# Attention with 128-row table products, signs split on ScalarE, and high halves read in place

## The chip, the cores and the metric

The kernel runs on one core of a Trainium2 chip. The metric is the device time of one execution in microseconds (us), the median over several runs. In the text PE is TensorE, PEld its weight loads, DVE is VectorE, ACT is ScalarE, POOL is GpSimd and SP is SyncE. A q behind an engine's name (PEldq, DVEq) means its instruction queue: the part that handles waits, register operations and the issue of instructions.

## The reference

One layer of a model that fuses image and text tokens: a tokenizer (sines and cosines of the image), attention, and a soft mixture of experts, for 8 batches of 640 tokens (512 image, 128 text) of width 192. The change is in the attention, which is linear attention with 4 sets of queries (G = 4), 12 heads and 64 dimensions:

```python
def _phi(x):
    return jnp.concatenate([jax.nn.relu(x), jax.nn.relu(-x)], axis=-1)
...
q = jnp.einsum('gbhnd,gde->gbhne', q, Wt) + bt[:, None, None, None, :]
q = jax.nn.gelu(q, approximate=False)
q = _ln(q, gt[:, None, None, None, :], betat[:, None, None, None, :])
qf = _phi(q) / jnp.sqrt(jnp.float32(2 * DH))
kf = _phi(k)
kv = jnp.einsum('bhnd,bhnm->bhdm', kf, v)
out = jnp.einsum('gbhnd,bhdm->gbhnm', qf, kv)
ksum = kf.sum(axis=2)
norm = jnp.einsum('gbhnd,bhd->gbhn', qf, ksum)
out = out / (norm[..., None] + 1e-06)
out = out.transpose(1, 3, 0, 2, 4).reshape(b, n, G * INNER)
fused = jax.nn.gelu(_ln(out @ Wf + bf, gf, betaf), approximate=False)
return fused @ Wo + bo
```

The features of a head are 128 numbers: 64 of the positive part and 64 of the negative part. For each batch and head there is a table `kv` of 128 x 64, and `ksum` as its 65th column (KVW = 65).

## The kernel before

The kernel is written engine by engine; each engine has its own order of work, and semaphores tie them together. Stages follow each other: tokenizer, attention weights, keys and values, attention, experts. Wherever a product needs nearly full precision, an f32 operand is split into two bf16 parts, `hi` and `lo` (the rest), and the product is made of three: hi x hi, hi x lo and lo x hi.

Keys and values (`keys_and_values`): for each of 40 tiles of 128 tokens (5 a batch) and each half of the heads, ACT makes the two signs of the key features (`kf`, layout head, sign, dimension), DVE and POOL split them, and `accumulate` on PE sums the tables in `ps_kv`. A product there has 128 tokens as rows and 64 feature columns (one head, one sign); two heads use the two column halves of the array. At a batch's end `store_kv` on ACT and DVE writes both parts of the tables to `kvs`, which holds all 8 batches: [batch, part, pair of heads, sign, 65], with one head of the pair in partitions 0 to 63 and the other in 64 to 127.

Attention (`attend`): 40 tiles of 128 tokens, and for each 6 octets j = 0 to 5 of 8 (set, head) pairs. Every engine walks through slots (tile, j) and in each slot does parts of several octets, so that the work is pipelined over some six slots. The first two tiles and the last are written out, the 37 between are a loop over a register `t`. An engine's order in one slot is written by hand:

- PE: `queries(j+3)` (5 products of 512 columns), at j = 2 `turn_x`, `turn_octet(j)` (4 transposes of the scaled queries into `ps_t`), at j = 4 `turn_y` (6 transposes), `attend_octet(j-1)` (the table products), `fuse(j-2)` (24 products of 384 columns), `turn_outputs(j-1)`, at j = 5 `project_out` (18 products).
- ACT: `high_outputs(j-2)`, `gelu(j+3)`, at j = 2 `move_x`, `features(j)`, `square(j+2)`, at j = 4 `fused_gelu` twice.
- DVE: `center(j+2)`, `low_outputs(j-2)`, `sum_q(j+3)`, `divide(j-1)`, `scale_q(j+1)`, `high_phi(j)`, `sum_squares(j+2)`, and parts for the tile at some j.
- POOL: `rstd_q(j+1)`, at j = 3 `rstd_y`, at j = 5 `low_ys`, `low_phi(j)`.
- SP: for each tile one DMA that copies the batch's tables from `kvs` to the fixed place `kv_now`.

The features of an octet go through these steps: `features` (ACT, from `ps_t` to `phi`, f32, one operation for each sign and each query set in the octet; octets 1 and 4 hold two sets), `high_phi` (DVE, copy to bf16), `low_phi` (POOL, the rest), `attend_octet` (PE). In `ps_t` two heads share the partitions, one in 0 to 63 and one in 64 to 127, so a table product has 64 rows, and the two heads of a pair run in the two row halves of the array: 4 pairs x 2 signs x 3 parts x 2 heads = 48 products of 65 columns. PE waits there for `phi_hi_done`, `phi_lo_done` and `o_done`, and for `kv_in` at j = 0.

The tokenizer already reads the high half of an f32 value as its upper 16 bits, every other bf16 element (`high`), as weights at L154.

## Time and profile before

| | |
|---|---|
| median of 3 runs | 2717.93 us (2717.76 to 2718.2) |
| profiled execution | 2718.29 us |
| its span, first to last instruction | 2716.4 us |
| mean granted TensorE clock, share of full speed | 0.96 |
| PE busy / DVE busy | 94% / 91% |
| ACT busy / POOL busy | 51% / 50% |

Busy times are those of instructions in execution; register, branch and semaphore operations in the queues are not counted. Products on PE are pipelined: one begins before the one ahead has ended, so the distance of their starts tells the pace, not their duration. In a timeline, a line with xN is N instructions of one kind that follow each other. A wait is put down to what came last.

### The profile page before, as it was taken

To read this page: it belongs to the slowest core of one execution; us is meant where nothing else is said; L and a number is where in the kernel's file an instruction comes from. 1 tells how busy PE (TensorE), PEld (TensorE's weight loads), DVE (VectorE), ACT (ScalarE), POOL (GpSimd) and SP (SyncE) were. 2 spreads that over 40 slices of the span, in tenths; PEclk is the share of its full clock that TensorE was granted. 3 is DMA by queue.
4 is the path that set the end of the run, shared out by engine and by line. 5 is a ranking of instruction groups with operands and counts; after the bars stand their busy time and mean duration, and the time that the engine had idled before them with its cause. 6 is when DMAs were issued, how large, how long until landed. Compare 5 with 4: busy or idle time off the path is not lost. (4 is left out here: it accounts for less than half of the span.)

```text
span 2716.4 us, 74938 instructions
## 1 busy us (share of the span) xinstructions
PE 2542.6 (94%) x29336; PEld 1722.5 (63%) x29336; DVE 2483.3 (91%) x3770; ACT 1392.7 (51%) x2302; POOL 1350.4 (50%) x1019
## 2 busy tenths in 40 slices
PE   4999999788879999999999999999999999999577
PEld 2777777555546666666666666666666666666335
DVE  6999999888889999999999999999999999999583
ACT  5676766555545545545444545545444544554231
POOL 0000000555556666666666666666666766666210
PEclk8999999899989999999999999999999999999765
DMA  7321210211100000000000000000000000000001
GB/s 153 96 51 36 51 35 18 62 36 41 35 7 14 10 8 12 6 12 6 12 6 12 6 12 12 6 12 6 12 6 12 6 12 12 6 12 7 6 0 58
DMA packets 45139, 62.39 MB, mean 23 GB/s; under 512 B 4416, under 2 KB 36160, under 8 KB 44760
## 3 DMA queue, kind: packets, MB, share of 16 engines
q1 hardware_dynamic: 43928, 61.07, 8.5%
q8 instruction: 40, 0.66, 0.1%
q10 hardware_dynamic: 1152, 0.51, 0.1%
q14 instruction: 19, 0.16, 0.0%
HBM read 41.66 MB, written 3.93 MB: 17 GB/s over the span
## 5 line engine op out<-in xcount | busy, mean ns | idle before, releaser
L1231 POOL TENSOR_TENSOR phi_lo<-phi,phi_hi 128x1024 bf16<-128x1024 f32 x240 | 511.2, 2130 | 459.8 <-DVE phi_hi L1112 459.8
L1022 ACT ACTIVATE o_hi<-ps_u 128x512 bf16<-128x512 f32 x240 | 143.3, 597 | 705.1 <-PE ps_u L927 705.1
L941 PE MATMUL ps_y<-staging,o_hi 128*128 128x384 bf16 x1920 | 470.4, 327 | 9.6 <-DVE o_lo L1134 1.9
L941 PE MATMUL ps_y<-staging,o_lo 128*128 128x384 bf16 x1920 | 469.0, 326 | 0.0
L941 PE MATMUL ps_y<-wf_lo,o_hi 128*128 128x384 bf16 x1920 | 468.9, 326 | 0.0
L1224 POOL TENSOR_TENSOR q_ssq<-q_ssq,half 128x8 f32<-128x8 f32 x240 | 405.9, 1691 | 18.8
L1013 ACT ACTIVATE phi<-ps_t,betat,gt 128x512 f32<-128x512 f32 (+1 forms) x640 | 384.8, 672 | 0.8 <-PE ps_t L896 0.8
L1090 DVE SCALAR_TENSOR_TENSOR shared<-q_sum,shared 128x512 f32<-128x512 f32 x240 | 374.3, 1559 | 1.4
L154 PE MATMUL acc<-w_b,feat 128*128 128x384 bf16 x1728 | 295.5, 331 | 42.8 <-DVE w_b L266 39.4
L154 PEld LDWEIGHTS acc<-w_b,feat 128*128 128x128 bf16 x1728 | 168.5, 99 | 158.3 <-DVE w_b L266 40.0
L941 PEld LDWEIGHTS ps_y<-staging,o_lo 128*128 128x128 bf16 x1920 | 187.8, 98 | 124.2
L941 PEld LDWEIGHTS ps_y<-wf_lo,o_hi 128*128 128x128 bf16 x1920 | 187.6, 98 | 124.5
L941 PEld LDWEIGHTS ps_y<-staging,o_hi 128*128 128x128 bf16 x1920 | 169.3, 98 | 118.7 <-issue 15.4
L252 DVE TENSOR_TENSOR f_low<-feat 128x4608 bf16<-128x4608 f32 x48 | 237.7, 4951 | 1.3 <-ACT feat L196 1.3
L369 POOL MEMSET half<- 128x40 f32 x1 | 0.1, 131 | 476.7 <-POOLq L101 476.7
L997 ACT ACTIVATE shared<-ps_a 128x512 f32<-128x512 f32 x240 | 143.5, 598 | 179.1 <-PE ps_a L880 176.1
L1112 DVE CAST phi_hi<-phi 128x1024 bf16<-128x1024 f32 x240 | 219.6, 915 | 0.0
L914 PE MATMUL ps_o<-kv_now,phi_hi 64*128 64x65 bf16 x7680 | 212.8, 191 | 1.7 <-issue 1.7
L914 PEld LDWEIGHTS ps_o<-kv_now,phi_hi 64*128 64x128 bf16 x7680 | 183.9, 94 | 42.1 <-issue 42.1
L914 PE MATMUL ps_o<-kv_now,phi_lo 64*128 64x65 bf16 x3840 | 202.8, 190 | 0.0
L1085 DVE TENSOR_REDUCE q_sum<-shared 128x8 f32<-128x512 f32 x240 | 162.5, 677 | 20.7 <-ACT shared L997 19.5
L914 PEld LDWEIGHTS ps_o<-kv_now,phi_lo 64*128 64x128 bf16 x3840 | 180.6, 94 | 0.0
(218 smaller groups left out, 5664.4 us busy)
## 6 DMA issues: line engine op xcount, KB each, us to landing
kv_now<-kvs SPq DMA_DIRECT2D x40, 390.0 KB, 2.6
xt<-in_x_dram SPq DMA_DIRECT2D x32, 320.0 KB, 5.5
wf_f<-in_wf_dram SPq DMA_DIRECT2D x24, 384.0 KB, 3.2
xt<-in_x_dram SPq DMA_DIRECT2D x32, 256.0 KB, 6.0
out_dram<-h SPq DMA_DIRECT2D x8, 480.0 KB, 2.9
staging<-in_wq_t_dram SPq DMA_DIRECT2D x1, 3072.0 KB, 11.0
staging<-in_tok_w_dram SPq DMA_DIRECT2D x12, 192.0 KB, 8.8
staging<-in_kv_w_dram SPq DMA_DIRECT2D x1, 1536.0 KB, 15.3
```

The costliest lines, as they stand in the source:

```text
L154: last = nc.tensor.matmul(acc[:, u, t, 0:2 * DIM], high(ring(u, i))[:, k, t * P:(t + 1) * P], w_b[:, i, k, :], start=i == 0 and k == 0, st ...
L252: nc.vector.tensor_tensor(low[:, r], feat[:, r], high(r), ALU.subtract).then_inc(low_ready, 1)
L914: last = nc.tensor.matmul(ps_o[:, a, i * KVW:(i + 1) * KVW], feature[rows, j % 2, sign, i * P:(i + 1) * P], kv_now[rows, table, pair, sign ...
L941: last = nc.tensor.matmul(ps_y[:, n, 0:HC], lhs, w[part][:, c, n * HC:(n + 1) * HC], start=c == 0 and lhs is oh and part == 'wf_hi', stop= ...
L997: nc.scalar.activation(q[:, j % RING].rearrange("p h d -> p (h d)"), ps_a[:, bank[f"oct{j}"], 0:OC], ACT.Gelu).then_inc(s["gelu_done"], 1)
L1013: last = nc.scalar.activation(phi[:, j % 2, sign, a * P:b * P], ps_t[:, a * P:b * P], ACT.Relu, bias=w['betat'][:, sign, g:g + 1], scale=w ...
L1022: nc.scalar.activation(o_hi[:, j % 2], ps_u[:, 0:OC], ACT.Copy).then_inc(s["o_hi_done"], 1)
L1085: nc.vector.tensor_reduce(total[:, j % 2], q[:, j % RING], AX_X, ALU.add).then_inc(s["q_sum"], 1)
L1090: nc.vector.scalar_tensor_tensor(out=q[:, j % RING], in0=total[:, j % 2].unsqueeze(2).broadcast_to([P, OCT, DH]), scalar=1.0 / DH, in1=q[: ...
L1112: nc.vector.tensor_copy(phi_hi[:, j % 2], phi[:, j % 2]).then_inc(s["phi_hi_done"], 1)
L1224: nc.gpsimd.tensor_tensor(ssq[:, j % 2], ssq[:, j % 2], w['half'][:, 0:OCT], ALU.pow).then_inc(s["q_rstd"], 1)
L1231: nc.gpsimd.tensor_tensor(phi_lo[:, j % 2], phi[:, j % 2], phi_hi[:, j % 2], ALU.subtract).then_inc(s["phi_lo_done"], 1)
```

## The change

Five edits that belong together:

- One head's two signs lie in the 128 partitions instead of two heads' one sign. A table is [128 features, 65] for each head, in `kv_hi` and `kv_lo` (two tensors now, [batch, head, 65]). `accumulate` takes 128 feature columns in one product (18 a call instead of 36), `attend_octet` takes 128 rows (24 instead of 48).
- `features` writes each sign to its own half of the partitions. An operation now covers one head of the pairs (64 partitions) and one sign: 4 for each query set in the octet, of the same number of columns as before.
- `phi_hi` is no tensor of its own: it is `phi` read as bf16, every other element. `high_phi` on DVE and its semaphore go; `low_phi` waits for `phi_done`, and `features` waits for `attended` of two octets earlier.
- `kv_now` and its DMA go. The products read `kv_hi[:, b, hd, :]` and `kv_lo[:, b, hd, :]`, with `b` worked out from the tile; in the looped tiles it is a run-time value.
- `o` is laid out by halves of the octet, and `divide` and `turn_outputs` index it so.

```diff
@@ keys_and_values: accumulate
-                    for j in range(HH // 2):
-                        for sign in range(2):
-                            for n, (k, v) in enumerate(((kf_hi, v_hi), (kf_hi, v_lo), (kf_lo, v_hi))):
-                                for side in range(2):
-                                    c = 2 * j + sign
-                                    last = nc.tensor.matmul(
-                                        ps_kv[side * DH:(side + 1) * DH, hf, c * KVW:(c + 1) * KVW],
-                                        k[:, m, 2 * j + side, sign, :], v[:, m, 2 * j + side, :],
...
+                    for j in range(HH):
+                        for n, (k, v) in enumerate(((kf_hi, v_hi), (kf_hi, v_lo), (kf_lo, v_hi))):
+                            last = nc.tensor.matmul(ps_kv[:, hf, j * KVW:(j + 1) * KVW],
+                                                    k[:, m, j].rearrange("p s d -> p (s d)"), v[:, m, j, :],
...
@@ attend: tensors
-        kv_now = sb("kv_now", [P, 2, HP, 2, KVW], BF16)
-        phi = sb("phi", [P, 2, 2, PAIRS * P], F32)
-        phi_hi = sb("phi_hi", [P, 2, 2, PAIRS * P], BF16)
-        phi_lo = sb("phi_lo", [P, 2, 2, PAIRS * P], BF16)
-        o = sb("o", [P, PAIRS, 2, DH], F32)
+        phi = sb("phi", [P, 2, PAIRS, 2, P], F32)
+        phi_hi = phi[:, :, :, :, :].bitcast(BF16)[:, :, :, :, 1::2]
+        phi_lo = sb("phi_lo", [P, 2, PAIRS, 2, P], BF16)
+        o = sb("o", [P, 2, PAIRS, DH], F32)
@@ attend: the block of SP with kv_now's DMA goes
@@ attend: attend_octet
-                    pe.wait_ge(s["phi_hi_done"], count(tile, j, NO))
                     pe.wait_ge(s["phi_lo_done"], count(tile, j, NO))
                     if (n := earlier(tile, j, NO, 1)) is not None:
                         pe.wait_ge(s["o_done"], n)
-                    if j == 0:
-                        pe.wait_ge(s["kv_in"], 16 * count(tile, 0, 1))
-                    for i in range(PAIRS):
-                        pair = (PAIRS * j + i) % HP
-                        for sign in range(2):
-                            for n, (feature, table) in enumerate(((phi_hi, 0), (phi_hi, 1), (phi_lo, 0))):
-                                for a in range(2):
-                                    rows = slice(a * DH, (a + 1) * DH)
-                                    last = nc.tensor.matmul(
-                                        ps_o[:, a, i * KVW:(i + 1) * KVW],
-                                        feature[rows, j % 2, sign, i * P:(i + 1) * P], kv_now[rows, table, pair, sign, :],
...
+                    b = batch_of(tile.t)
+                    for i in range(OCT):
+                        hd = (OCT * j + i) % HEADS
+                        c = i % PAIRS
+                        out = ps_o[:, i // PAIRS, c * KVW:(c + 1) * KVW]
+                        ph, pl = (v[:, j % 2, i // 2, i % 2, :] for v in (phi_hi, phi_lo))
+                        nc.tensor.matmul(out, ph, kv_hi[:, b, hd, :], start=c == 0, stop=False, skip_group_check=True)
+                        nc.tensor.matmul(out, ph, kv_lo[:, b, hd, :], start=False, stop=False, skip_group_check=True)
+                        last = nc.tensor.matmul(out, pl, kv_hi[:, b, hd, :], start=False, stop=c == PAIRS - 1,
+                                                skip_group_check=True)
@@ attend: features
-                        act.wait_ge(s["phi_hi_done"], n)
-                        act.wait_ge(s["phi_lo_done"], n)
-                    for sign in range(2):
-                        for g, a, b in groups(j):
-                            last = nc.scalar.activation(
-                                phi[:, j % 2, sign, a * P:b * P], ps_t[:, a * P:b * P], ACT.Relu,
-                                bias=w['betat'][:, sign, g:g + 1], scale=w['gt'][:, sign, g:g + 1])
+                        act.wait_ge(s["attended"], n)
+                    for g, a, b in groups(j):
+                        for head in range(2):
+                            rows = slice(head * DH, (head + 1) * DH)
+                            for sign in range(2):
+                                last = nc.scalar.activation(
+                                    phi[sign * DH:(sign + 1) * DH, j % 2, a:b, head, :],
+                                    ps_t[rows, a * P:b * P].rearrange("p (i n) -> p i n", n=P), ACT.Relu,
+                                    bias=w['betat'][rows, sign, g:g + 1], scale=w['gt'][rows, sign, g:g + 1])
@@ attend: high_phi goes, low_phi
-                    nc.vector.tensor_copy(phi_hi[:, j % 2], phi[:, j % 2]).then_inc(s["phi_hi_done"], 1)
...
-                    pool.wait_ge(s["phi_hi_done"], count(tile, j, NO))
+                    pool.wait_ge(s["phi_done"], count(tile, j, NO))
@@ early_fusion_kernel
-            kvs = sa("kvs", [P, BATCH, 2, HEADS // 2, 2, KVW], BF16)
-            kv_hi, kv_lo = kvs[:, :, 0], kvs[:, :, 1]
+            kv_hi = sa("kvs_hi", [P, BATCH, HEADS, KVW], BF16)
+            kv_lo = sa("kvs_lo", [P, BATCH, HEADS, KVW], BF16)
```

## Rows read from the trace of the kernel before

**Rows 1.** The page's head and part 1: busy us (share of the span) x instructions.

```profile
span 2716.4 us, 74938 instructions
...
PE 2542.6 (94%) x29336; PEld 1722.5 (63%) x29336; DVE 2483.3 (91%) x3770; ACT 1392.7 (51%) x2302; POOL 1350.4 (50%) x1019
```

**Rows 2.** Windows, two stages: us; PE, PEld, DVE, ACT, POOL busy; clock; DMA.

```profile
490.00:763.00 273.00, 230.82 (x3818) 151.15 (x3817) 223.44 (x505) 146.07 (x337) 150.48 (x140) 0.92 0.11 35
763.00:2540.00 1777.00, 1748.59 (x21437) 1181.16 (x21438) 1694.55 (x2639) 874.04 (x1681) 1173.12 (x843) 0.99 0.02 9
```

**Rows 3.** Timeline, PE, one slot: start us, us, engine, line, operation, tiles, shapes, count.

```profile
1522.61 0.60 PE L896 MATMUL ps_t<-ident,z 128*128 128x128 f32 x4
1523.14 0.24 PE L914 MATMUL ps_o<-kv_now,phi_hi 64*128 64x65 bf16 x4
...
1523.86 0.19 PE L914 MATMUL ps_o<-kv_now,phi_lo 64*128 64x65 bf16 x2
1523.99 0.50 PE L941 MATMUL ps_y<-staging,o_hi 128*128 128x384 bf16 x2
```

**Rows 4.** Timeline, PE: `turn_octet` of j = 4, 5, 0, 2, 3.

```profile
1499.82 0.60 PE L896 MATMUL ps_t<-ident,z 128*128 128x128 f32 x4
...
1507.51 0.60 PE L896 MATMUL ps_t<-ident,z 128*128 128x128 f32 x4
...
1515.80 0.60 PE L896 MATMUL ps_t<-ident,z 128*128 128x128 f32 x4
...
1529.63 0.60 PE L896 MATMUL ps_t<-ident,z 128*128 128x128 f32 x4
...
1536.57 0.60 PE L896 MATMUL ps_t<-ident,z 128*128 128x128 f32 x4
```

**Rows 5.** Timeline, ACT: `features` of j = 1 and j = 2.

```profile
1523.30 1.93 ACT L1013 ACTIVATE phi<-ps_t,betat,gt 128x256 f32<-128x256 f32 x4
...
1530.53 1.43 ACT L1013 ACTIVATE phi<-ps_t,betat,gt 128x512 f32<-128x512 f32 x2
```

**Rows 6.** Timeline, POOL: `low_ys`, and `low_phi` of j = 0.

```profile
1510.75 1.95 POOL L1244 TENSOR_TENSOR ys_lo<-shared,ys_hi 128x768 bf16<-128x768 f32 x1 [1.70 <-DVE ys_hi L1163]
...
1520.26 2.13 POOL L1231 TENSOR_TENSOR phi_lo<-phi,phi_hi 128x1024 bf16<-128x1024 f32 x1 [2.48 <-DVE phi_hi L1112]
```

**Rows 7.** Source lines, PE's queue: duration ns min/median/max, first and last start us.

```profile
L905 PEldq EVENT_SEMAPHORE  x1: 2139/2139/2139, 1520.3 to 1520.3; - x1
...
L907 PEldq FUSED_REGOPS  x1: 37/37/37, 1522.5 to 1522.5; - x1
...
L933 PEldq EVENT_SEMAPHORE  x1: 51/51/51, 1523.6 to 1523.6; - x1
...
L871 PEldq EVENT_SEMAPHORE  x1: 51/51/51, 1533.5 to 1533.5; - x1
...
L894 PEldq EVENT_SEMAPHORE  x1: 51/51/51, 1533.8 to 1533.8; - x1
```

**Rows 8.** Source line L1069, DVE's queue, whole run.

```profile
L1069 DVEq FUSED_REGOPS  x111: 65/65/105, 870.0 to 2444.5; - x111
```

**Rows 9.** Groups by line: count, busy us, mean ns, idle before, releaser.

```profile
L1112 DVE CAST phi_hi<-phi 128x1024 bf16<-128x1024 f32 x240 | 219.6, 915 | 0.0
...
L914 PEld LDWEIGHTS ps_o<-kv_now,phi_hi 64*128 64x128 bf16 x7680 | 183.9, 94 | 42.1 <-issue 42.1
...
L154 PEld LDWEIGHTS acc<-w_b,feat 128*128 128x128 bf16 x1728 | 168.5, 99 | 158.3 <-DVE w_b L266 40.0 <-ACT feat L195 7.4 <-issue 6.9
...
L896 PE MATMUL ps_t<-ident,z 128*128 128x128 f32 x960 | 144.9, 274 | 3.1 <-DVE z L1104 3.1
...
L163 PEld LDWEIGHTS acc<-w_b,f_low 128*128 128x128 bf16 x1728 | 144.0, 98 | 6.1
...
L692 POOL TENSOR_TENSOR kf_lo<-kf,kf_hi 128x384 bf16<-128x384 f32 x80 | 90.8, 1134 | 62.5 <-DVE kf_hi L638 62.5
```

More of the change, by code:

```diff
@@ L523, in accumulate @@
                     m = KBUF[2 * t + hf]
[L524 to L533 removed]
+                    for j in range(HH):
+                        for n, (k, v) in enumerate(((kf_hi, v_hi), (kf_hi, v_lo), (kf_lo, v_hi))):
+                            last = nc.tensor.matmul(ps_kv[:, hf, j * KVW:(j + 1) * KVW],
+                                                    k[:, m, j].rearrange("p s d -> p (s d)"), v[:, m, j, :],
+                                                    start=t == 0 and j == 0 and n == 0,
+                                                    stop=t == TPB - 1 and j == HH - 1 and n == 2, skip_group_check=True)
                     last.then_inc(summed, 1)
@@ L585, in store_kv @@
                     act.wait_ge(summed, 2 * TPB * b + 2 * (TPB - 1) + hf + 1)
-                    nc.scalar.activation(kv_hi[:, b, hf * PH:(hf + 1) * PH].rearrange("p h s d -> p (h s) d"),
+                    nc.scalar.activation(kv_hi[:, b, hf * HH:(hf + 1) * HH, :],
                                          ps_kv[:, hf, 0:HH * KVW].rearrange("p (h d) -> p h d", h=HH),
@@ L647, in store_kv @@
                     dve.wait_ge(kv_hi_ready, 2 * b + hf + 1)
-                    nc.vector.tensor_tensor(kv_lo[:, b, hf * PH:(hf + 1) * PH].rearrange("p h s d -> p (h s) d"),
+                    nc.vector.tensor_tensor(kv_lo[:, b, hf * HH:(hf + 1) * HH, :],
                                             ps_kv[:, hf, 0:HH * KVW].rearrange("p (h d) -> p h d", h=HH),
-                                            kv_hi[:, b, hf * PH:(hf + 1) * PH].rearrange("p h s d -> p (h s) d"),
+                                            kv_hi[:, b, hf * HH:(hf + 1) * HH, :],
                                             ALU.subtract).then_inc(kv_lo_ready, 1)
@@ L705, in _, with attend @@
                     batch(b, False)
-def attend(nc, w, shared, kvs, stats, h, ident):
+def attend(nc, w, shared, kv_hi, kv_lo, stats, h, ident):
     OCT = 8
@@ L759, in attend @@
         ps_y = ctx.enter_context(nc.psum_tensor("ps_y", [P, 2, 512], F32))
-        names = ("kv_in xe_zero xe_one x_norm x_turned xh_ready xe_ready xl_ready "
+        names = ("xe_zero xe_one x_norm x_turned xh_ready xe_ready xl_ready "
                  "queries gelu_done q_sum centered squared q_ssq_s q_var q_rstd q_scaled "
-                 "q_turned phi_done phi_hi_done phi_lo_done attended den_done rec_done o_done "
+                 "q_turned phi_done phi_lo_done attended den_done rec_done o_done "
                  "o_turned o_hi_done o_lo_done fused y_moved y_bn_s y_aggr y_var y_rstd y_norm "
@@ L854, in attend @@
         with nc.Block() as block:
-            @block.sync
-            def _(sp):
-                def tables(tile):
-                    if (n := earlier(tile, NO - 1, NO, NO)) is not None:
-                        sp.wait_ge(s["attended"], n)
-                    sp.dma_start(kv_now[:, :, :, :, :], kvs[:, batch_of(tile.t)]).then_inc(s["kv_in"], 16)
-                tables(Tile(0))
-                with sp.Fori(1, TILES) as t:
-                    tables(Tile(t))
             @block.tensor
@@ L1106, in scale_q @@
                                             ALU.mult).then_inc(s["q_scaled"], 1)
-                def high_phi(tile, j):
-                    dve.wait_ge(s["phi_done"], count(tile, j, NO))
-                    if (n := earlier(tile, j, NO, 2)) is not None:
-                        dve.wait_ge(s["attended"], n)
-                    nc.vector.tensor_copy(phi_hi[:, j % 2], phi[:, j % 2]).then_inc(s["phi_hi_done"], 1)
                 def divide(tile, j):
@@ L1200, in slot @@
                         scale_q(of, k)
-                    if tile.real:
-                        high_phi(tile, j)
                     of, k = octet(tile, j + 2)
@@ L1801, in early_fusion_kernel @@
             keys_and_values(nc, a, w, kv_hi, kv_lo, stats, h, ident)
-            attend(nc, w, shared, kvs, stats, h, ident)
+            attend(nc, w, shared, kv_hi, kv_lo, stats, h, ident)
         soft_experts(nc, a, out, h, ident)
```

9 lines of the change are left out of this document (2 added, 7 removed).

## The prediction

> **What bounds the kernel now.** I read the busy line of the page first. TensorE (PE) is 94% busy and VectorE (DVE) 91%, ScalarE (ACT) and GpSimd (POOL) about half [rows 1]. Then the stretches: keys and values take 273 us with PE at 85%, and the attention stage 1777 us with PE at 98% and DVE at 95% [rows 2]. So the attention stage decides, and there both leading engines look full. The timeline of PE tells them apart: it goes from one group of products to the next with no wait for an operand. A table product begins when the transposes before it are through, a `fuse` when the table products are [rows 3]. So PE waits for nothing that DVE does, however full DVE is. PE's order of work is the path that sets the end; its slots of one octet last 6.81, 7.02, 6.94, 6.99, 7.69 and 8.29 us, 43.74 us a tile: read the starts of `turn_octet` [rows 3, 4]; that of j = 4 comes again one tile later, at 1543.56.
>
> **The change, part by part.**
>
> 1. Table products on PE. Now an octet has 24 pairs of 64-row products; eight groups of three pairs run from 1523.14 to 1523.86, the last pair included at its start, so 23 intervals take 0.72 us, 0.031 us a pair [rows 3]. After, 24 single 128-row products of the same 65 columns. The trace has no 128-row product as short. I take the same 0.031 us, since two loads and two products fit into that interval now and one of each will have to. The ends change too: the four transposes follow each other at 0.109 us (the group spans 0.60 us [rows 3], one lasts 274 ns [rows 9]), so the products could start at 1523.05 and start at 1523.14; and the `fuse` starts at 1523.99 where the next pair would have been at 1523.89. That is 0.09 + 0.10 = 0.19 us an octet lost at the change between 64-row and 128-row products, and it goes: 240 x 0.19 = 46 us gained. In keys and values 80 `accumulate` calls lose their column halves in the same way, at most 15 us; PE is idle for 15% of that stage [rows 2], so I count half, 8 us. Together 54 us. If both gaps have another cause, it is 0.
>
> 2. Strided high halves as weights. The weight load from every other 16 bits at L154 takes 99 ns, the one from packed data at L163 98 ns [rows 9]: nothing, and both lie beside a product.
>
> 3. `high_phi` leaves DVE: 0.9 us of DVE per octet, 219.6 us in all [rows 9]. DVE sets nothing, so it is worth 0 by itself. It also stood between ACT and POOL, so `low_phi` can start as soon as the features are there.
>
> 4. Signs split on ScalarE. Now one octet of one group has 2 operations of 512 columns (1.43 us together), one of two groups (j = 1 and 4) 4 of 256 (1.93 us) [rows 5]. After, they are 4 and 8, of 64 rows but the same columns. At 0.67 and 0.45 us for each further one that is 2.8 and 3.75 us. ACT is at 49% in this stage [rows 2]; 1.4 or 1.8 us more per slot fit.
>
> 5. `low_phi` on POOL: 2.13 us [rows 6], its second input now strided. Kept at 2.13; the dearest elements of a POOL subtraction here are L692's, 1134 ns for 384, which would make 3.0 us.
>
> 6. The table read at a run-time position. `kv_now` and its DMA (already off every path) go, and each product of PE reads `kv_hi` or `kv_lo` at an address that depends on the loop's tile. Such an address is computed by a register operation on the engine's own queue. DVE's two instructions of `normalize_x` have three of them in each of the 37 looped tiles [rows 8], so I count one for each new address: 8 heads x 2 tables = 16 an octet, behind the wait for `phi_lo_done`. Their price: on PE's queue four single operations (L871, L872, L851, L894) start between 1533.5 and 1533.8 [rows 7], 0.1 us apart, though each is busy for at most 51 ns. That is 1.6 us. The loads and products themselves pass that queue in at most 0.011 us: 96 of them between 1522.5 and 1523.6 [rows 7]; 48 x 0.011 = 0.5 us. A product with a register address is not in this trace: its extra lies between 0 and one such operation, 0.1 us. I take 0.04, nearer the plain product, so 24 x 0.04 = 1.0 us. Together 3.1 us per octet (bounds 2.1 and 4.5) from the wait to the last product, where the array needs 0.7.
>
> Today PE's queue hides such things, since it stands at this wait long ahead of the array: at 1520.3 for products of 1523.14. But it stands there until 1522.44, just behind the end of `low_phi` at 1522.39 [rows 6, 7]. So what counts is from that release to the moment when the array would want the last product. Counted from `turn_octet`'s start: features begin at 0.7 [rows 4, 5], and the release is at 0.7 + 2.8 + 2.13 = 5.6 us (6.6 for j = 1 and 4; 5.85 for j = 2, where `move_x` is ahead and features begin at 0.9; 7.3 for j = 5, where `low_ys` is ahead on POOL until 5.2 [rows 6]). The last product is due at the next slot's start, less 0.19, plus 0.44 for the transposes and 0.69 for 23 products: 7.75, 7.96, 7.88, 8.58 (`turn_y`'s six transposes are ahead, 0.65), 8.63 and 9.23 for j = 0 to 5. The cover is 2.1, 1.35, 2.0, 2.9, 2.0 and 1.9 us. With 3.1 us the queue is late by 1.0 + 1.75 + 1.1 + 0.2 + 1.1 + 1.2 = 6.35 us a tile. 37 tiles are looped (the three written out have fixed addresses): 235 us. What queues behind is everything else on PE, `fuse` first, so this adds to the span.
>
> The sum: 2716.4 + 235 - 54 = 2897; outside the span lie 1.9 us (2718.29 profiled, 0.4 above the median of the runs), so 2899; I say 2900. At 2.1 us of issue the lateness is 1.15 a tile, 43 us, and the result 2707; at 4.5 us it is 14.75 a tile, 546 us, 3210.
>
> The rule that speaks most plainly on item 6 is in the Trainium skill, "TensorE: Matmul & The Clock Gate", section on what happens when you issue a matmul: a product that the sequencer's own program has to handle costs it about 62 ns. If a register address brings that about, the extra is some 0.05 us, and an estimate from it is 2943 us. No row here shows it.
>
> **The rivals.**
>
> - The queue stays ahead (the other side). If these register operations take only the time that they are busy, at most 51 ns, 16 take 0.8 us; with 0.5 for the rest, 1.3 us is within every cover. It decides at 1.35 us for j = 1. Then only item 1 is left: 2664, or 2657 with all of the keys' gain. For it: the busy times, and the long lead of PE's queue. Against: the four starts. Chance 0.2.
>
> - It cancels: 2.1 us of issue gives 2707, 2.2 us gives 2725, so between them it is no change. That means within 0.2% (5 us), about what a measurement of this kernel can tell. Chance 0.08.
>
> - POOL's chain: the subtraction with the strided input takes 3.0 us. All covers lose 0.9; with 2.1 us of issue the lateness is 5.75 a tile, 213 us, 2877; with 3.1 us it is 11.75 a tile, 435 us, 3099. For it: nothing but that no POOL row has such a stride. Chance 0.12.
>
> - Loads not hidden behind 65 columns. The rows show 0.031 us for a pair, each array half loading and multiplying once in it. If a full load and its product went one after the other, each 0.031, 24 would add 0.74 an octet, 179 us, and with the 54 gained and no lateness the time is 2843. Chance 0.08. The same page of the Trainium skill, section on the back-to-back issue gap, has 81 ns in a stream of loads and products of 128 columns where the product alone has some 56; an estimate with its excess of 25 ns is 2808 us.
>
> **How the numbers follow.** The forecast (register addresses make PE's queue late, 2.3 to 4.5 us of issue) has 0.52 and its own range is 2740 to 3210. With the two other slow rivals slower has 0.72, same 0.08, faster 0.2. The range for 8 in 10: from 2665, since a tenth may lie below, to 3200.
>
> **What would show it.** The idle time before the table products' loads, now 42 us in all [rows 9], grows to over 200, most in the slots behind j = 1 and least behind j = 3, in looped tiles and not in the first two. PE's queue has some 16 register operations an octet at this line. `low_phi` starts within 0.1 us of the last feature and keeps 2.13 us; features take 2.8 and 3.75 us. The 0.09 and 0.10 us around the products vanish in the first tiles. DVE loses its 0.9 us per octet. Wrong would be: register operations closer than 0.05 us, or a queue that computes them before the wait.

## The result, and the profile of the changed kernel

The changed kernel takes 2770.58 us (median of 4 runs, 2769.68 to 2771.37) against 2717.85 of the kernel before beside it: ratio 1.0194, 95% interval 1.0176 to 1.0212. It is slower, by 53 us and not by the 182 forecast.

The page's head and part 1 ([rows 1] has those of before), and the windows of the same two stages (before: [rows 2]):

```profile
span 2767.7 us, 61832 instructions
...
PE 2522.7 (91%) x22136; PEld 1740.9 (63%) x22136; DVE 2073.6 (75%) x3530; ACT 1884.6 (68%) x2942; POOL 1305.3 (47%) x1019
```

```profile
490.00:763.00 273.00, 220.25 (x2401) 150.81 (x2399) 228.68 (x516) 150.77 (x345) 153.85 (x145) 0.92 0.11 35
763.00:2540.00 1777.00, 1699.62 (x15301) 1171.39 (x15302) 1257.40 (x2344) 1337.24 (x2271) 1103.32 (x822) 1.00 0.00 0
```

In the attention stage ACT's busy time rose from 874 to 1337 us, DVE's fell from 1695 to 1257, and PE, which has fewer products now, stands idle for 77 us in place of 28. Where it stands idle, the waits of 31 looped tiles (1000 to 2400 us) say: engine, line, releaser, us in total, times, longest.

```profile
DVE q_ssq L1080 <- ACT shared L984: 240.2, 155, 2.8
...
PE ps_a L871 <- DVE xn L1051: 29.3, 31, 1.0
...
PE ps_a L860 <- ACT shared L1019: 21.0, 31, 0.7
```

In every tile PE waits for `normalize_x` ahead of `turn_x` (L871) and for `fused_gelu` ahead of a `queries` (L860). The kernel before has no such wait in the same window. The timeline around the first, PE, then ACT, then DVE, then POOL (start us, us, then as in [rows 3]):

```profile
1544.48 0.38 PE L864 MATMUL ps_a<-q_lo,xe 128*128 128x512 bf16 x1
1545.81 0.43 PE L871 MATMUL ps_a<-ident,xn 128*128 128x128 f32 x2 [0.95 <-DVE xn L1051]
1546.08 0.60 PE L880 MATMUL ps_t<-ident,z 128*128 128x128 f32 x4
```

```profile
1538.80 4.56 ACT L994 ACTIVATE phi<-ps_t,betat,gt 64x256 f32<-64x256 f32 x8
1543.39 0.63 ACT L984 ACTIVATE shared<-shared 128x512 f32<-128x512 f32 x1
```

```profile
1540.61 0.68 DVE L1086 TENSOR_TENSOR z<-shared,q_ssq 128x512 f32<-128x512 f32 x1
1544.05 0.69 DVE L1080 TENSOR_REDUCE q_ssq<-shared 128x8 f32<-128x512 f32 x1 [2.75 <-ACT shared L984]
1544.65 1.02 DVE L1051 TENSOR_SCALAR xn<-h,stats 128x192 f32 x2
```

```profile
1543.44 1.89 POOL L1205 TENSOR_TENSOR phi_lo<-phi 128x1024 bf16<-128x1024 f32 x1 [4.20 <-ACT phi L994]
```

Read it backwards. `turn_x` begins 1.33 us behind the last query product, where 0.22 would do. It waits for `normalize_x`, whose operands were there long ago, but which stands in DVE's queue behind `sum_squares` (L1080). That one stood idle 2.75 us for `square` (L984), which stands on ACT behind the eight feature operations: 4.56 us in place of 1.93 [rows 5]. A part of the wait is `normalize_x` itself: it takes longer than its own time here, since it starts while POOL's `low_phi` runs (1543.44 to 1545.33); e16 has the size.

The run-time addresses show in the few places where table products are 0.12 instead of 0.03 us apart. PE's queue at L895 in one octet, and in the 31 tiles; L896 in the same octet; then the last products of that octet:

```profile
L895 PEldq FUSED_REGOPS  x8: 46/46/112, 1530.6 to 1532.3; - x8
```

```profile
L895 PEldq FUSED_REGOPS  x618: 46/46/112, 1001.9 to 2399.7; - x155
```

```profile
L896 PEldq ALU_OP  x8: 32/32/32, 1530.8 to 1532.5; - x8
```

```profile
1532.18 0.20 PE L895 MATMUL ps_o<-kvs_hi,phi 128*128 x1
1532.29 0.19 PE L896 MATMUL ps_o<-kvs_lo,phi 128*128 x1
1532.32 0.19 PE L897 MATMUL ps_o<-kvs_hi,phi_lo 128*128 x1
1532.45 0.20 PE L895 MATMUL ps_o<-kvs_hi,phi 128*128 x1
1532.56 0.19 PE L896 MATMUL ps_o<-kvs_lo,phi 128*128 x1
```

Two register operations for a head (one for each table), 16 in 1.9 us (1530.6 to 1532.5), 0.12 us apiece. But only 618 at L895 in 31 tiles, 20 a tile, and as many at L896: 40 a tile, not 96. An address that the loop's body has already computed for this tile is not computed again. The 40 fit 16 operations for octet 5, which in this loop belongs to the tile before and so has its own addresses, 16 for octet 0, 8 for octet 1 and none for the rest. The third product of a head (L897) has none of its own, since it uses the address of the first.

To see all gaps at once, this table has the distances of `turn_octet`'s starts, mean over 34 looped tiles of each profile; column j is the time from `turn_octet` of j to the next, so the wait ahead of `turn_x` is in column 1, the one ahead of `queries` in column 4. "Median" is that of the runs, with the ratio to the kernel before beside it and its 95% interval. The experiments follow below. e1 and e17 leave out the sorting of heads and signs, and e16 three quarters of the low parts; in all others nothing is left out.

| kernel | 0 | 1 | 2 | 3 | 4 | 5 | tile | median | ratio |
|---|---|---|---|---|---|---|---|---|---|
| before | 6.81 | 7.03 | 6.93 | 6.99 | 7.69 | 8.29 | 43.73 | 2717.85 | 1 |
| changed | 7.13 | 7.97 | 7.18 | 6.59 | 8.32 | 8.16 | 45.34 | 2770.58 | 1.0194 (1.0176 to 1.0212) |
| e1 | 7.02 | 6.81 | 6.59 | 6.67 | 7.47 | 8.07 | 42.63 | 2664.40 | 0.9803 (0.9787 to 0.9820) |
| e2 | 6.59 | 7.96 | 7.18 | 6.59 | 8.31 | 8.16 | 44.79 | 2751.33 | 1.0127 (1.0110 to 1.0144) |
| e3 | 7.15 | 6.81 | 7.40 | 7.55 | 8.32 | 8.16 | 45.39 | 2771.68 | 1.0205 (1.0188 to 1.0222) |
| e4 | 7.13 | 7.96 | 7.18 | 6.59 | 7.66 | 9.38 | 45.90 | 2791.25 | 1.0277 (1.0260 to 1.0294) |
| e5 | 7.14 | 6.81 | 7.45 | 8.15 | 7.80 | 8.16 | 45.51 | 2782.62 | 1.0243 (1.0226 to 1.0260) |
| e6 | 6.59 | 6.81 | 7.30 | 8.30 | 7.81 | 8.16 | 44.98 | 2765.20 | 1.0172 (1.0155 to 1.0189) |
| e7 | 6.81 | 8.45 | 7.18 | 6.99 | 7.84 | 8.29 | 45.55 | 2787.73 | 1.0258 (1.0241 to 1.0275) |
| e8 | 6.81 | 7.03 | 6.81 | 6.81 | 7.69 | 8.29 | 43.44 | 2706.61 | 0.9956 (0.9940 to 0.9973) |
| e10 | 6.82 | 7.49 | 7.18 | 7.41 | 7.83 | 8.29 | 45.02 | 2764.75 | 1.0176 (1.0159 to 1.0193) |
| e11 | 7.17 | 6.81 | 7.25 | 7.12 | 8.31 | 8.89 | 45.55 | 2778.43 | 1.0224 (1.0206 to 1.0241) |
| e12 | 6.59 | 6.81 | 7.08 | 7.30 | 8.32 | 8.89 | 44.99 | 2756.84 | 1.0146 (1.0129 to 1.0162) |
| e14 | 6.60 | 6.81 | 6.63 | 6.59 | 7.66 | 10.00 | 44.29 | 2729.99 | 1.0049 (1.0032 to 1.0065) |
| e15 | 6.59 | 6.81 | 6.63 | 6.59 | 7.66 | 9.19 | 43.47 | 2699.28 | 0.9935 (0.9921 to 0.9949) |
| e16 | 6.59 | 7.55 | 7.18 | 6.59 | 8.32 | 8.16 | 44.39 | 2737.12 | 1.0075 (1.0059 to 1.0091) |
| e17 | 6.59 | 6.81 | 6.59 | 6.67 | 7.47 | 8.07 | 42.21 | 2649.71 | 0.9753 (0.9739 to 0.9766) |
| e18 | 7.13 | 7.49 | 7.18 | 6.59 | 7.84 | 8.16 | 44.38 | 2730.43 | 1.0051 (1.0034 to 1.0068) |
| e19 | 6.59 | 6.81 | 6.59 | 6.59 | 7.55 | 8.83 | 42.96 | 2678.86 | 0.9859 (0.9843 to 0.9876) |
| e20 | 7.13 | 7.97 | 7.18 | 6.59 | 8.32 | 8.16 | 45.35 | 2770.44 | 1.0197 (1.0180 to 1.0214) |

The changed kernel loses 45.34 - 43.73 = 1.61 us a tile, x 37 = 60 us, and gains about 7 ahead of the first tile: that accounts for the 53. Column 3 is the one to look at for the products: in the changed kernel nothing waits there, and it fell from 6.99 to 6.59. Of these 0.40 us the products have 0.22; the other 0.18 go with `high_phi` (e8: 6.81).

### The profile page after: what moved, and what is told of

It reads as the page before. It is cut to its first block and busy times, and to the rows that moved or that the text cites. A ratio compares the mean times of both kernels' runs of the same rounds, so it can differ in the third digit from the quotient of the medians.

```text
span 2767.7 us, 61832 instructions
## 1 busy us (share of the span) xinstructions
PE 2522.7 (91%) x22136; PEld 1740.9 (63%) x22136; DVE 2073.6 (75%) x3530; ACT 1884.6 (68%) x2942; POOL 1305.3 (47%) x1019
## 5 line engine op out<-in xcount | busy, mean ns | idle before, releaser
L994 ACT ACTIVATE phi<-ps_t,betat,gt 64x512 f32<-64x512 f32 (+1 forms) x1280 | 852.0, 666 | 14.4 <-PE ps_t L880 0.3
L1205 POOL TENSOR_TENSOR phi_lo<-phi 128x1024 bf16<-128x1024 f32 x240 | 491.1, 2046 | 523.0 <-ACT phi L994 523.0
L1198 POOL TENSOR_TENSOR q_ssq<-q_ssq,half 128x8 f32<-128x8 f32 x240 | 413.2, 1722 | 18.8
L1080 DVE TENSOR_REDUCE q_ssq<-shared 128x8 f32<-128x512 f32 x240 | 164.7, 686 | 306.9 <-ACT shared L984 306.9
L1110 DVE TENSOR_TENSOR o_lo<-ps_u,o_hi 128x512 bf16<-128x512 f32 x240 | 165.0, 687 | 92.9 <-ACT o_hi L1004 92.8
L895 PE MATMUL ps_o<-kvs_hi,phi 128*128 (+1 forms) x1920 | 220.4, 196 | 1.5 <-POOL phi_lo L1205 1.3
L896 PE MATMUL ps_o<-kvs_lo,phi 128*128 (+1 forms) x1920 | 219.4, 193 | 0.0
L897 PE MATMUL ps_o<-kvs_hi,phi_lo 128*128 (+1 forms) x1920 | 218.6, 193 | 0.0
L1072 DVE SCALAR_TENSOR_TENSOR shared<-q_sum,shared 128x512 f32<-128x512 f32 x240 | 209.8, 874 | 1.4
```

Of the source, the lines that this page charges most:

```text
L895: nc.tensor.matmul(out, ph, kv_hi[:, b, hd, :], start=c == 0, stop=False, skip_group_check=True)
L896: nc.tensor.matmul(out, ph, kv_lo[:, b, hd, :], start=False, stop=False, skip_group_check=True)
L897: last = nc.tensor.matmul(out, pl, kv_hi[:, b, hd, :], start=False, stop=c == PAIRS - 1, skip_group_check=True)
L994: last = nc.scalar.activation(phi[sign * DH:(sign + 1) * DH, j % 2, a:b, head, :], ps_t[rows, a * P:b * P].rearrange("p (i n) -> p i n", n ...
L1072: nc.vector.scalar_tensor_tensor(out=q[:, j % RING], in0=total[:, j % 2].unsqueeze(2).broadcast_to([P, OCT, DH]), scalar=1.0 / DH, in1=q[: ...
L1080: nc.vector.tensor_reduce(ssq[:, j % 2], sq, AX_X, ALU.add).then_inc(s["q_ssq_s"], 1)
```

## The experiments

The diffs are shortened: `...` stands for what is left out, and calls are written with the octet they work on.

**Which cost is it?** Theory S: the doubled feature operations make ACT late. Theory R, the prediction's: the addresses make PE's queue late.

e1, two feature operations over all 128 partitions again:

```diff
-for head in range(2):
-    rows = slice(head * DH, (head + 1) * DH)
-    for sign in range(2):
-        ... phi[sign * DH:(sign + 1) * DH, j % 2, a:b, head, :], ps_t[rows, a * P:b * P] ...
+for head in range(2):
+    ... phi[:, j % 2, a:b, head, :], ps_t[:, a * P:b * P] ...
```

> The changed kernel with as many feature operations on ScalarE as before: two per octet and query set over all 128 partitions, one for each place of a head pair. It leaves out the sorting of heads and signs into their rows, so its output is another; the table products, their run-time addresses and all else stay. In the changed kernel TensorE waits in each looped tile 1.11 us for the turned x (behind the last query product 1.33 instead of 0.22 us), 0.84 us at the queries behind slot 4, and the fuse of slot 2 begins 0.43 instead of 0.03 us behind the table products. Theory S (the doubled feature operations make ScalarE late, and these three waits are its price): they vanish, 2.0 to 2.35 us a tile x 37 = 74 to 87 us, so 2684 to 2697 us. Rival R (the run-time addresses on TensorE's queue are the loss, as the prediction had it): nothing changes, 2770 us, and the three waits stay. Rival D (the waits come from VectorE's new order without high_phi): 2770 us as well, with the same waits.

2664.4 us, 106 less than the changed kernel and 20 below the range that S had given. Both waits and the gap in column 2 are gone; only column 0 still shows the register operations (7.02, without them 6.59). R falls as the main cause: the addresses are all still there.

e2, fixed addresses:

```diff
+sp.dma_start(kv_now[:, :, :, :], kvs[:, batch_of(tile.t)]).then_inc(s["kv_in"], 16)
...
-nc.tensor.matmul(out, ph, kv_hi[:, b, hd, :], ...)
+nc.tensor.matmul(out, ph, kv_now[:, 0, hd, :], ...)
```

> The changed kernel with kv_now back: one DMA a tile copies the batch's tables to a fixed place, and the 24 products of an octet have fixed addresses. Nothing is left out. Rival R: the loss is the addresses: the time falls by 51 us and more, below 2720 us. Theory S: only the gaps of about 0.1 us between table products go, in slot 0 (0.24 + 0.23 us and 0.07 behind the last product) and slot 2 (0.12 + 0.07 us), 0.73 us a tile x 37 = 27 us, so about 2744 us; 2770 if the late ScalarE sets the pace of the tile anyway, since a wait that ends at a fixed time of another engine takes up what is gained ahead of it.

2751.3 us: 19 less, all of it in column 0 (7.13 to 6.59). Column 2 didn't move, although its register operations went: the `fuse` there begins 0.62 us behind the table products in place of 0.43, so it waits for something else.

**One call moved.** e3 puts `normalize_x` ahead of `sum_squares` on DVE, e4 `fused_gelu` ahead of `square` on ACT:

```diff
 # e3, VectorE's slot
+if j == 1 and nxt.real: normalize_x(nxt)
 if of.real: sum_squares(of, k)
...
-if j == 1 and nxt.real: normalize_x(nxt)
```

> The changed kernel with one call moved: normalize_x stands ahead of sum_squares in VectorE's order of slot 1. sum_squares waits there for square, which stands on ScalarE behind the eight feature operations; normalize_x itself has its operands long before. Theory S: the 1.11 us before the turned x vanish, and part of the 0.40 us behind the table products of slot 2, so 41 to 56 us less, 2715 to 2730 us. If VectorE as a whole is late there (rival D), the wait shrinks by less than half, above 2750 us. Rival R: 2770 us.

> The changed kernel with one call moved: fused_gelu (six operations, which free two banks of ps_a) ahead of square in ScalarE's order of slot 4. Theory S: the bank comes free 0.63 us earlier (one square), so of the 0.84 us at the queries behind slot 4 0.2 stay: 23 us less, 2747 us. Rival: square is then 2.1 us later, and its chain (sum of squares, POOL's power, scale_q, transposes) takes up the gain: within 5 us of 2770. Rival R: 2770 us, since the waits at the queries are no part of the loss.

Both moves did in their own column what they were to do (e3: 7.97 to 6.81; e4: 8.32 to 7.66), and neither gained: 2771.7 and 2791.3 us. The loss came back behind it: for e3 in columns 2 and 3 (7.40 and 7.55), for e4 in column 5 (9.38). Waits of e4:

```profile
PE ps_y L921 <- DVE o_lo L1110: 34.4, 30, 1.1
```

The `fuse` now waits for `low_outputs`, which stands behind `sum_squares`, which waits for the `square` that e4 had made later. In e3 DVE's `scale_q` began inside POOL's `low_phi` (from 1503.14) and took over three times its 0.68 us:

```profile
1503.23 2.35 DVE L1086 TENSOR_TENSOR z<-shared,q_ssq 128x512 f32<-128x512 f32 x1
1505.51 0.67 DVE L1080 TENSOR_REDUCE q_ssq<-shared 128x8 f32<-128x512 f32 x1
```

**Take `square` off ACT.** e5 makes it a `scalar_tensor_tensor` on DVE, right ahead of `sum_squares`; e6 has fixed addresses too.

> The changed kernel with square moved from ScalarE to VectorE (one scalar_tensor_tensor of 512 columns right ahead of sum_squares); nothing is left out. With ScalarE's feature operations back at their old number the changed kernel took 2664.4 us, and moving single calls brought nothing: the wait at the turned x came back one slot later behind the table products (0.03 to 1.00 us), the one at the queries behind the next table products (0.12 to 1.34 us), each time because VectorE stood at sum_squares for a square that was late. Theory S2 (ScalarE's late square blocks VectorE's queue, whatever stands behind it): with square on VectorE the 1.11 and 0.40 us go, and 0.63 of the 0.84 us at the queries, since fused_gelu starts one square earlier: 2.1 us a tile x 37 = 79 us, 2692 us. Rival V (VectorE can't carry 0.7 to 1.2 us more a slot, the higher value where it meets GpSimd's subtraction): low_outputs is late for the fuse in most slots, 2760 us or more.

> The run before this one with kv_now and its DMA back, so with fixed table addresses as well; nothing is left out. The fixed addresses alone brought the changed kernel 19 us (2770.6 to 2751.3, slot 0 0.54 us shorter, slot 2 not shorter since its fuse waited for another). Theory S2: here slot 2 gains as well, 0.73 us a tile, 27 us: 2665 us, below both kernels. Rival V: 2735 us or more.

2782.6 and 2765.2 us: in the ranges of rival V (DVE has no room for one more operation), though the `fuse` waits in column 3 only (e6: 2 and 3) and not in most slots. `turn_x` is in time (6.81), but DVE's new operation meets POOL's subtraction; DVE, then POOL, of e5:

```profile
1509.29 2.38 DVE L1071 SCALAR_TENSOR_TENSOR shared<-shared 128x512 f32<-128x512 f32 x1
1511.71 0.69 DVE L1079 TENSOR_REDUCE q_ssq<-shared 128x8 f32<-128x512 f32 x1
```

```profile
1508.93 2.20 POOL L1205 TENSOR_TENSOR phi_lo<-phi 128x1024 bf16<-128x1024 f32 x1 [1.36 <-ACT phi L988]
```

DVE's operation ends 0.54 us behind `low_phi` (1511.67 and 1511.13), after 2.38 us for work of 0.68, and the `fuse` of column 3 (8.15) waits behind it.

**Parts of the change in the kernel before.** e7 only cuts its feature operations in two, e8 only reads the high halves in place, e10 does both.

```diff
 # e7, ScalarE
-phi[:, j % 2, sign, a * P:b * P], ps_t[:, a * P:b * P], ...
+phi[rows, j % 2, sign, a * P:b * P], ps_t[rows, a * P:b * P], ...   # for head in range(2)
 # e8
-phi_hi = sb("phi_hi", [P, 2, 2, PAIRS * P], BF16)
+phi_hi = phi[:, :, :, :].bitcast(BF16)[:, :, :, 1::2]
```

> The kernel before with each feature operation cut into two of 64 rows (4 and 8 an octet as in the changed kernel), same layout, same result; nothing else. Theory S2: the doubled operations alone make the kernel before slower, by what leaving them out took from the changed one, 106 us (2770.6 - 2664.4), so about 2825 us, with the waits at turn_x, at the queries and behind the table products; more if high_phi, which stands in VectorE's queue behind the features, adds to it. Rival I (the waits need the run-time addresses or the new layout too): below 2760 us.

> The kernel before with the features' high halves read in place, as every other 16 bits of phi, and high_phi left off VectorE; all else as before, nothing left out. The prediction's parts 2, 3 and 5: no change, 2713 to 2723 us, with low_phi at 2.13 us and the weight loads at 98 us ns as from packed data. Rival: VectorE's 0.9 us an octet were worth something, since the gaps of 0.26 and 0.32 us behind the table products of slots 2 and 3 wait for low_outputs: 0.14 + 0.20 us a tile x 37 = 13 us less, 2705 us. Other rival: strided weights cost each load some ns: over 2725 us.

> The kernel before with two parts of the change, high halves read in place (alone 2706.6 us) and each feature operation cut into two of 64 rows (alone 2787.7 us); products stay 64-row with fixed addresses; nothing left out. It stands between the kernel before and the changed one with fixed addresses (2751.3 us). Additive: 2707 + 70 = 2777 us. If high_phi, which stood in VectorE's queue behind the late features, was a part of the 70 us: 2750 to 2765 us. The 128-row products are then worth the difference to 2751.3 us; if TensorE's waits end at fixed times of other engines they are worth only the 11 us of keys and values and a part of the rest.

e7 takes 2787.7 us: the cut alone costs 70 us, with no run-time address and no new layout, and column 1 holds 1.42 of its 1.82 us a tile. That is neither the 106 of e1 nor the rival's time below 2760: the cut is enough for a loss, and the new layout or the addresses add to it. e8 takes 2706.6, 11 less: the prediction had 0 for this, the rival 13. Columns 2 and 3 fell by 0.12 and 0.18 us, where the `fuse` began 0.26 and 0.32 us behind the table products and now begins 0.12 behind them, as everywhere. So in the kernel before PE did wait a little, behind a DVE that had `high_phi` to do; the slot of [rows 3] is one where it did not. e10 takes 2764.8: 58 above e8, 12 less than additive, as expected if `high_phi` behind the late features had a part in e7's 70.

**Is it the order alone?** Theory Q: it is the order of the calls. Rival P: DVE's operations are held up by POOL's subtraction. Rival L: the sums of squares come too late. e11 moves `sum_squares` behind `low_outputs` of the next slot, e12 adds fixed addresses, e14 also puts both ahead of `center` and `fused_gelu` ahead of `square`, e15 also puts `high_ys` ahead of `sum_squares` and `low_ys` ahead of `rstd_q`.

```diff
 # e15, VectorE's slot
+low_outputs(j - 2)
+if j == 5: high_ys(prev)
+sum_squares(j + 1)
 center(j + 2)
-low_outputs(j - 2)
...
-if j == 5: high_ys(prev)
 scale_q(j + 1)
-sum_squares(j + 2)
```

> The changed kernel with one call moved: sum_squares stands in VectorE's order behind low_outputs of the next slot instead of at the end of its own; nothing left out. Theory Q (VectorE's queue stands at sum_squares for ScalarE's late square, and low_outputs and normalize_x, whose operands are there, stand behind it): the 1.11 us before the turned x and the 0.40 us in slot 2 go, the 0.84 us at the queries stay, since they are ScalarE's own: 56 us less, 2715 us. Rival P (the part of the loss is GpSimd's subtraction, in which VectorE's operations from SBUF to SBUF take up to 1.8 us longer): center and normalize_x still meet it, so at most half comes back, above 2740 us. Rival L: the sums are now so late that scale_q holds the transposes, and it is slower, above 2771 us.

> The same with fixed table addresses (kv_now and its DMA back); nothing left out. Theory Q: 27 us less again, 2688 us, below the kernel before; only the wait at the queries is left. Rival P: 2715 us or more. Rival L: above 2750 us.

> Fixed table addresses and three moves in the orders: sum_squares as in the last two, low_outputs and sum_squares ahead of center on VectorE, fused_gelu ahead of square on ScalarE; nothing left out. Theory Q: fused_gelu's move, which alone cost 20 us because sum_squares waited for the square behind it ahead of low_outputs, now gains its 0.63 us a tile, 23 us: 2665 us. Rival P: low_outputs is out of reach of center, which meets GpSimd's subtraction, but normalize_x isn't: about 2690 us. Rival L: above 2750 us.

> The last version (fixed addresses and three moves in the orders, 2730.0 us) with two more moves in slot 5: high_ys ahead of sum_squares on VectorE, low_ys ahead of rstd_q on GpSimd; nothing left out. In the last version slots 0 to 3 last 6.60, 6.81, 6.63 and 6.59 us, as without any wait, and nearly all that is lost lies in slot 5, 10.0 instead of 8.07 us, 1.32 of it before project_out, which waits for ys_lo, 0.6 before the fuse. Theory Q (the loss is order alone): ys_lo is there 1.2 us earlier or more, the wait of project_out goes, 49 us less: 2681 us, below the kernel before. Rival L: POOL's power for the next octet is then 2 us late, scale_q holds the transposes of slot 0, and no more than half comes back, above 2705 us; it also shows as a longer slot 0.

One call moved again brought nothing (e11: 2778.4, and with fixed addresses e12: 2756.8, both in rival L's range; column 1 fell to 6.81, 3 and 5 rose). In column 5 `project_out` now waits for `ys_lo`, which POOL does behind the late power of `rstd_q`; e11:

```profile
PE ps_a L942 <- POOL ys_lo L1218: 17.5, 31, 0.6
```

All together they did, though neither e14 nor e15 reached the time that theory Q had asked for (2665 and 2681): 2730.0, then 2699.3 us, 18 below the kernel before and 52 below e2, which has the fixed addresses too, though no operation of ACT was saved. Columns 0 to 2 are within 0.04 us of e17's, and column 3 is 0.08 shorter: that is what the moves on DVE gained. Those of e15 took 0.81 us from column 5. `fused_gelu`'s move isn't shown to be one: column 4 is 7.66, as in e4, but columns 4 and 5 together are 17.04 us in e4, 17.66 in e14 and 16.85 in e15, against 16.48 in the changed kernel. e15 without it was not run.

**What POOL's subtraction does.** e16 subtracts a quarter of the columns.

> The changed kernel with a quarter of low_phi: GpSimd subtracts 256 of 1024 columns (the low parts of the other pairs stay zero, so that part of the result is left out). It takes about 0.5 instead of 1.9 us. TensorE itself never waits for low_phi, so by theory Q alone nothing changes: 2765 to 2771 us. Theory P: VectorE's operations from SBUF to SBUF end only when low_phi does (center 1.22 instead of 0.69 us when it starts inside one, in 76 of 224 cases; normalize_x 0.80 us); without that the turned x comes 0.4 us earlier and the fuse of slot 2 too: 15 to 40 us less, 2730 to 2755 us.

2737.1 us, 33 less, in the range of theory P; but only half of it is P's. `normalize_x` in e16, its two operations; in the changed kernel, where the first starts inside `low_phi` each time, that takes 796 ns:

```profile
L1051 DVE TENSOR_SCALAR xn<-h,stats 128x192 f32 x37 | 13.7, 371 | 0.0
L1051 DVE TENSOR_SCALAR xn<-h,stats 128x64 f32 x37 | 11.4, 308 | 0.0
```

Column 1 gives 0.42 of the 0.95 us a tile, just what `normalize_x` saves: 16 us of the 33. The other 0.54 are in column 0 and were not expected: `low_phi` of octet 5 takes 1.06 us in place of 2.35 and is done 1.3 us earlier, so PE's queue comes to its 16 register operations earlier and hides them, as with fixed addresses (6.59).

**The products by themselves.** e17 is e1 with fixed addresses.

> The changed kernel with the old number of feature operations (as in the first experiment, their sorting by head and sign left out, 2664.4 us) and fixed table addresses: what the 128-row products and the halves in place are worth with neither of the other two costs. There the register operations cost 0.43 us a tile, in slot 0 alone (7.02 instead of 6.59 us), 16 us: 2648 us. That would be 58 us below the kernel before with halves in place (2706.6 us), where the prediction had 54 for the products. If a register address also cost something inside each product, 2635 us or less.

2649.7 us, as expected. Against e8, which has the old products, the 128-row ones are worth 57 us, in attention and in keys and values together.

**The order of feature operations.** e18 has the two query sets innermost, e20 the heads innermost, e19 is e15 with the order of e18.

```diff
-for g, a, b in groups(j):
-    for head in range(2):
-        for sign in range(2):
+for head in range(2):
+    for sign in range(2):
+        for g, a, b in groups(j):
```

> The changed kernel with the loops of features in another order: the two query sets of octets 1 and 4 innermost, so that two operations on the same rows follow each other; same operations, nothing left out. In the changed kernel an operation of 256 columns begins 0.573 us behind the one ahead of it, one of 512 columns 0.786; in the kernel before, on 128 rows, 0.45 and 0.66; with the halves in the old layout 0.45 within a row half and 0.56 to 0.57 across. Theory O (following operations overlap by 0.11 us only on the same rows): features of octets 1 and 4 take 4 x 0.11 = 0.46 us less, 4.1 instead of 4.56 us, those of the others stay at 3.12; both waits behind them (1.11 and 0.84 us) shrink by as much: 0.92 us a tile, 34 us, 2737 us. Rival: the overlap is lost because of the layout of phi, whatever the order: 4.56 us and 2770 us.

> The changed kernel with sign outside and head inside in the loops of features: following operations write the same rows of phi and read other rows of ps_t in half of the cases; same operations, nothing left out. If it is the rows written that decide about the overlap of 0.11 us, features take 0.23 us less in the single octets (2.9 instead of 3.12) and 0.46 less in octets 1 and 4, and the time is about 2737 us or a little less. If the rows read decide as well, nothing changes: 3.12 and 4.56 us, 2770 us.

> The fastest version so far (fixed addresses, five moves in the orders, 2699.3 us) with the loops of features in that order as well; nothing left out. Its period is 43.47 us a tile against 42.21 without any wait (6.59, 6.81, 6.59, 6.67, 7.47, 8.07 us by slot), and 1.12 of the 1.26 us lie in slot 5, behind fused_gelu, which stands behind the features of octet 4. Theory O: 0.46 us less there, and the small waits of slots 2 and 4 go: 0.46 to 0.7 us a tile, 17 to 26 us: 2673 to 2682 us. Rival: another chain ends last there (VectorE's), 2695 to 2700 us.

The features of an octet with two sets, in e7, then e18, then e20:

```profile
1503.90 4.08 ACT L1015 ACTIVATE phi<-ps_t,betat,gt 64x256 f32<-64x256 f32 x8
```

```profile
1521.36 4.08 ACT L994 ACTIVATE phi<-ps_t,betat,gt 64x256 f32<-64x256 f32 x8
```

```profile
1515.85 4.56 ACT L994 ACTIVATE phi<-ps_t,betat,gt 64x256 f32<-64x256 f32 x8
```

e18 takes 2730.4 us, 40 less than the changed kernel for an exchange of loops, 0.48 us in columns 1 and 4 each. e20 changed nothing, 2770.4, so it is not the written rows alone that count. e19 takes 2678.9 us with nothing left out, 38 below the kernel before (ratio 0.9859, 0.9843 to 0.9876): it beats both kernels. What it still has over e17 lies in column 5, 8.83 against 8.07 (and 0.08 in column 4, which column 3 gives back).

## Why the prediction was wrong

Right in its sign, wrong in its size and in its reason, and the sign was luck: with the 19 us that the addresses did cost in place of 235, its own sum is some 2684 us, faster than before. e1 comes near that kernel: all the addresses, the old number of feature operations, 2664 us. Two steps failed, parts 4 and 6: the one that makes the kernel slower had been put at nothing, and the one that was to make it slower costs a twelfth of its forecast. By its own parts:

1. Table products: 54 us forecast, 57 shown (e8 to e17). A 128-row product follows at 0.03 us, and the gaps at the two ends went as described. Keys and values: the first `turn_octet` starts at 766.2 us on average in the 16 profiles with 128-row products and at 773.0 in the four without, 7 us for 8 forecast.
2. Strided weights: nothing, right. The loads take 97 ns at L895.
3. `high_phi` worth 0: wrong by 11 us (e8). PE's order did have two small waits behind DVE in each tile.
4. **The first step that failed, a term put at nothing.** "ACT is at 49% in this stage; 1.4 or 1.8 us more per slot fit." Two errors. The size: 3.12 and 4.56 us, not 2.8 and 3.75. And the reasoning: a share of the stage says how much work fits, not who stands behind it. I followed the features to `low_phi` and to the table products, where no wait came except behind octet 5, and not to `square` behind them on ACT, to `sum_squares` on DVE, which waits for it, and to `normalize_x` and `low_outputs`, which wait for nothing but their place behind `sum_squares`. The list of waits had to be made for all that is queued behind the lengthened step. It cost 58 us in the old layout (e8 to e10) and 106 in the new one (e1).
5. `low_phi` at 2.13 us: 2.05 on average, right. What it does to DVE while it runs was left out, 16 us here (e16).
6. **The second step that failed, a term mis-sized.** Addresses: 235 us forecast, 19 shown (e2). The price of one was nearly right, 0.12 us for 0.1. The number was wrong: 40 a tile for 96, since I counted the 16 of every octet as new, where the loop's body computes each once. The extra for a product with a register address, 0.04, is none: the first two products of a head, with their addresses known, follow at 0.03. The covers were the right idea: 16 operations cost 0.54 us for octet 5, nothing for octet 0, and nothing anywhere once `low_phi` is early (e16). The sign that was named for this part did not come: the idle time before the table products' loads went from 42 us to 9.5, and not to over 200. The rule of the Trainium skill, "TensorE: Matmul & The Clock Gate", section on what happens when you issue a matmul, that a product handled by the sequencer's program costs about 62 ns, doesn't come into play: products with register addresses follow at 30 ns here.

The parts don't add up, and that is the second lesson. In a ladder: before 2717.9, high halves in place 2706.6 (-11), operations cut 2764.8 (+58), 128-row products and new layout with fixed addresses 2751.3 (-13), run-time addresses 2770.6 (+19). The products are worth 57 us where PE leads, and 13 where ScalarE's late work sets the moment at which PE may go on: then a faster PE only waits longer. The columns say so too: in columns 1, 2 and 4, e10 and e18 are equal to 0.01 us, though e18 has the faster products. But more than this is in the 44 us that are missing. The feature operations lose their overlap in the new layout (last section). From e10 to e2 columns 0 and 5 fall by 0.23 and 0.13 us and column 3 by 0.82, where a wait of 0.6 us goes, but columns 1 and 4 grow by 0.47 and 0.48, and this is what e18 takes back: 0.95 us a tile, 35 us. e18 with fixed addresses, which would show the products without that loss, was not run.

## What to carry to other kernels

When an operation gets longer on an engine with room, list everything behind it in that engine's queue, everything that waits for those, and everything behind the waiters in theirs; the engine's busy share answers none of this. A wait that goes when one call is moved and returns in the next slot points to a queue held at its head: look for all calls that stand behind it, and move them together or not at all. And measure the parts of a change both alone and on top of each other before adding them up.

## What the runs showed of the hardware

- **ScalarE's following operations overlapped only on the same rows.** With 128 rows, or the same 64, an operation of 256 columns starts 0.45 or 0.46 us behind the last, one of 512 columns 0.66 to 0.68 us, which is 0.11 us before the last one ends. If the rows written change (changed kernel, in each step) or the rows read (e20), it is 0.57 and 0.79: the next one starts only when the last has ended, 0.12 us later. The Trainium skill, "ScalarE: Activation LUTs", section on what ACT_TABLE_LOAD costs, has "Back-to-back ACTIVATEs overlap by ≈ 93 ns"; here it is 0.11 us, and none where the rows change.
- **An operation of VectorE from SBUF to SBUF that starts inside GpSimd's subtraction ends only behind it.** With two inputs in SBUF it ends 0.55 us behind: `center` takes 0.68 us alone and 1.22 when it starts well inside `low_phi` (twice a tile in the changed kernel), `scale_q` and e5's `square` up to 2.38. The kernel before has more of this, two of three `center`s start inside and take 2.24 us in the median; its mean, before and after, is in the lines below. `normalize_x` has one such input and ends 0.12 us behind (371 ns alone, 796 in the changed kernel). Reductions (0.69 in both cases) and operations that read PSUM (0.69) are not touched. The Trainium skill, "SBUF — State Buffer", section on the two separate sides, says that VectorE and GpSimd share one pair of ports as an exclusive lock, held for the whole instruction, where VectorE's operation has two SBUF inputs or is in a two-port mode. For two inputs the trace agrees. Whether `normalize_x` is in such a mode, no run here shows.

```profile
L1090 DVE SCALAR_TENSOR_TENSOR shared<-q_sum,shared 128x512 f32<-128x512 f32 x240 | 374.3, 1559 | 1.4
```

```profile
L1072 DVE SCALAR_TENSOR_TENSOR shared<-q_sum,shared 128x512 f32<-128x512 f32 x240 | 209.8, 874 | 1.4
```

- **Register addresses on TensorE's queue** cost 0.12 us for each new address, behind the wait, and nothing when it comes up again in the loop's body. The array sees it only where the queue is late: 0.54 us a tile here.
